# First stage of an embedding, filter and expert kernel: gathers taken straight from the index table, in another order against the graph vectors

## The chip, the cores and the metric

The kernel runs on one core of a Trainium2 chip. Its time is the device time of one execution in microseconds (us), and lower is better. The core has a matrix engine (PE), a vector engine (DVE), an activation engine (ACT), GpSimd (POOL), which here issues the gathers, and SyncE (SP), which issues plain transfers. Each works through its own list of instructions in order. They meet only at semaphores: an instruction signals one when it is complete, and a waiting instruction holds up everything behind it on its engine. 16 DMA engines move the data that SP, ACT and POOL ask for.

## The reference

64 sequences of 128 tokens pass through a token and graph embedding with a layer norm, a long convolution, and a layer of eight experts with two chosen per token. Only the first stage is touched by the change. For each sequence:

```python
emb = word_emb[input_ids] + pos_emb                  # 128 x 192
def vgcn(ids, adj, W, b):                            # three graphs
    ev = word_emb[ids]                               # 128 x 192
    H = einsum('bgh,bhd->bgd', adj, ev)
    g = H.mean(axis=1)                               # a mean over the 128 rows
    return relu(g @ W.T + b)                         # 16 values
x = concat([emb, graphs broadcast over the tokens])  # 192 + 48
y = layernorm(x @ W_proj.T + b_proj) * gamma + beta  # 192
```

The mean of `adj @ ev` over its rows is the vector of column means of `adj`, times `ev`; the kernel computes it so. Later stages use `y` of all sequences.

## The kernel before

The first stage works in 16 groups of four sequences (`NQ = 16`, `Q = 4`), numbered 0 to 15 here, with two buffers `p` for everything that a group holds. A group needs 16 gathers of 128 rows each: four for the tokens (`emb_g`, L473) and four for each of the three graphs (`ev_g`, L478), so twelve. It also needs three plain loads of adjacency matrices (`adj_s`, L358).

PE does for a group, in this order: twelve products of an adjacency matrix with a column of 1/128, which give its column means (L560, signal `colsum`); eight transposes of the gathered token rows (L565, L566, signal `emb_t`); twelve products of a diagonal-like block of the means with the gathered graph rows, summed into a 12 x 192 tile (L575, signal `gvec`: the graph vectors); two small transposes of that tile (L580, L581, signal `gt`); the graph features (L585, signal `gfeat`); the projection (L592, L593, signal `proj`).

ACT copies between these steps: the means onto the diagonals (L759, waits `colsum`), the turned embeddings (L762, L763, waits `emb_t`), the graph vectors (L768) and their transposes (L770, L771), then the relu (L773). It also normalizes rows of a group (L780, after `ln_ready`), splits the weights of one expert per two groups into a high part (L787, L788) and stores the split weights (L324). DVE waits for `proj` and then does two layer norms of the group (`rows`, L977 to L993, signal `ln_ready`), with a drain (a wait for its own earlier writes) between dependent steps, and computes the low part of an expert (L999, L1000) once per two groups. SP loads the adjacency of group i+2 once `colsum` of group i is signalled, and the next expert's weights once the last store has landed.

POOL first waits for `gvec` of group i-2, copies the group's indices out of the table with one instruction (L469, from `ids_i` into `idx`), and then issues all 16 gathers of group i. Groups 0 and 1 have no wait. After group 15 the Toeplitz tiles of the convolution are loaded into the room of `ev_g` (SP waits for `gvec` of all groups, L391), and the convolution (L611) starts when ACT has written the rows of the last group.

## Time and profile before

| | |
|---|---|
| median of three runs | 1231.76 us (1229.6 to 1235.03) |
| the profiled execution | 1239.12 us, its span 1237.3 us |
| granted clock of PE in the span | 0.816 of full speed |
| PE, DVE, ACT, POOL busy in the span | 71%, 52%, 44%, 54% |
| first stage | from the start to about 513 us, where L611 begins |

The profiled execution is 7.4 us longer than the median of the runs shown. A row of a timeline gives start, duration, engine, line, operation, output and input with their count, and in brackets how long the engine was idle before it and what ended that. Ends of matrix products are modelled, so a row of PE tells when the product was started, and the row of whoever waits for it tells when its signal was there. "remote" means that the profile could not tie the end of a wait to an instruction that had just ended.

### The profile page before, as it was taken

The numbers are of one execution on the slowest core, as the hardware profiler recorded it, in microseconds if no ns is written. First come the engines' busy times: TensorE is split into PE (matmuls) and PEld (weight loads), VectorE is DVE, ScalarE is ACT, GpSimd is POOL, SyncE is SP. The second block draws the span as 40 slices with busy tenths as digits, with TensorE's granted clock in tenths as the row PEclk, the third lists the DMA queues.
The fourth block names the chain that finished last, engine by engine and source line by source line (L and its number), as shares of the span: only waits on it lengthen the run. The fifth ranks groups of instructions, "written<-read, shape, count | busy, mean of one in ns | idle before, by whom it ended". The sixth has DMA issues, their size and how long they took to land. (4 is left out here: it accounts for less than half of the span.)

```text
span 1237.3 us, 22985 instructions
## 1 busy us (share of the span) xinstructions
PE 878.2 (71%) x7442; PEld 775.1 (63%) x7442; DVE 639.1 (52%) x2223; ACT 540.3 (44%) x1323; POOL 674.0 (54%) x608
## 2 busy tenths in 40 slices
PE   1544444654444547495875799998988998999991
PEld 0433333443333435495874689998988998998991
DVE  2043434453534354537868745664655565655661
ACT  1021212121212123354855757665655766676760
POOL 6455554655554650002530057776866887878874
PEclk9966666666666667696556989998999999999996
DMA  6234343543535351591088054477477446434442
GB/s 202 74 106 143 108 143 116 147 156 96 163 87 168 95 178 36 144 285 55 1 233 270 3 169 80 59 169 178 57 176 213 62 94 162 62 56 62 62 52 30
DMA packets 119542, 146.94 MB, mean 119 GB/s; under 512 B 13476, under 2 KB 105799, under 8 KB 117415
## 3 DMA queue, kind: packets, MB, share of 16 engines
q0 software_dynamic: 39552, 53.26, 23.1%
q1 hardware_dynamic: 78902, 82.31, 21.8%
q10 hardware_dynamic: 1008, 10.34, 2.1%
q8 instruction: 46, 0.75, 0.3%
q14 instruction: 34, 0.27, 0.1%
HBM read 107.05 MB, written 38.82 MB: 118 GB/s over the span
## 5 line engine op out<-in xcount | busy, mean ns | idle before, releaser
L880 ACT ACTIVATE Hs<-bank,U 128x256 bf16<-128x256 f32 x426 | 211.9, 497 | 183.7 <-PE bank L708 154.0
L517 POOL DMA_INDIRECT out<-Hs,si x142 | 236.9, 1669 | 85.5 <-issue 85.2
L1202 DVE TENSOR_TENSOR Hs<-Hs 128x512 bf16<-128x512 f32 x213 | 147.5, 692 | 148.2 <-ACT Hs L881 134.5
L575 PE MATMUL bank<-ev_g,diag 128*12 128x192 f32 x384 | 96.1, 429 | 179.8 <-ACT diag L759 172.1
L478 POOL DMA_INDIRECT ev_g<-in_word_emb,idx x192 | 185.0, 964 | 58.5 <-issue 58.5
L508 POOL DMA_INDIRECT blob<-xtab_d,gi x142 | 149.0, 1049 | 123.5 <-DVE gi L1187 84.2
L881 ACT ACTIVATE Hs<-bank,U 128x256 f32<-128x256 f32 x426 | 214.0, 502 | 0.0
L723 PE MATMUL bank<-U,Hs 128*128 128x192 bf16 x852 | 213.0, 250 | 0.2 <-issue 0.2
L725 PE MATMUL bank<-U,Hs 128*128 128x192 bf16 x852 | 211.4, 248 | 0.0
L724 PE MATMUL bank<-U,Hs 128*128 128x192 bf16 x852 | 211.1, 248 | 0.0
L575 PEld LDWEIGHTS bank<-ev_g,diag 128*12 128x12 f32 x384 | 44.0, 118 | 231.7 <-issue 119.5
L759 ACT ACTIVATE diag<-bank 128x12 f32<-128x12 f32 x16 | 3.1, 192 | 275.1 <-remote 270.0
L704 PE MATMUL bank<-blob,U 128*128 128x256 bf16 x426 | 117.0, 275 | 1.6 <-DVE blob L1191 1.6
L706 PE MATMUL bank<-blob,U 128*128 128x256 bf16 x426 | 116.9, 274 | 0.0
L705 PE MATMUL bank<-blob,U 128*128 128x256 bf16 x426 | 116.9, 274 | 0.0
L707 PE MATMUL bank<-blob,U 128*128 128x256 bf16 x426 | 116.9, 274 | 0.0
L708 PE MATMUL bank<-blob,U 128*128 128x256 bf16 x426 | 116.9, 274 | 0.0
L724 PEld LDWEIGHTS bank<-U,Hs 128*128 128x128 bf16 x852 | 84.9, 100 | 0.2
L723 PEld LDWEIGHTS bank<-U,Hs 128*128 128x128 bf16 x852 | 83.9, 98 | 0.7 <-issue 0.4
L725 PEld LDWEIGHTS bank<-U,Hs 128*128 128x128 bf16 x852 | 83.6, 98 | 0.2
L977 DVE TENSOR_TENSOR ys<-bank,posb 128x384 f32<-128x384 f32 x32 | 16.3, 552 | 127.4 <-PE bank L593 117.7
L473 POOL DMA_INDIRECT emb_g<-in_word_emb,idx x64 | 62.4, 974 | 31.2 <-issue 19.6
(184 smaller groups left out, 1726.5 us busy)
## 6 DMA issues: line engine op xcount, KB each, us to landing
U<-blob_d SPq DMA_DIRECT2D x20, 771.0 KB
U<-blob_d SPq DMA_DIRECT2D x20, 672.0 KB
adj_s<-in_adj SPq DMA_DIRECT2D x48, 256.0 KB
ev_g<-kpad_d SPq DMA_DIRECT2D x24, 512.0 KB, 6.2
wst<-in_wsrc SPq DMA_DIRECT2D x8, 1344.0 KB
blob_d<-blob ACTq DMA_DIRECT2D x7, 1443.0 KB
xtab_d<-U SPq DMA_DIRECT2D x4, 1552.0 KB, 8.9
out<-Hs SPq DMA_DIRECT2D x4, 1536.0 KB, 10.9
```

The source lines that it names most:

```text
L478: pool.indirect_dma_start(ev_g[:, p, j, b, :], None, t["word_emb"], bass.IndirectOffsetOnAxis(ap=idx[:, p, k:k + 1], axis=0)).then_inc(ev_ ...
L508: pool.indirect_dma_start(xg_f[:, q % RX, h, :], None, xtab_d, bass.IndirectOffsetOnAxis(ap=gi[:, q % RX, h:h + 1], axis=0)).then_inc(xg_i ...
L517: pool.indirect_dma_start(out, bass.IndirectOffsetOnAxis(ap=si[:, q % RX, h:h + 1], axis=0), yo[:, q % RX, h, :], None, compute_op=ALU.add ...
L575: last = mm(bank[3][0:KG, 0:D], diag[:, p, k, :], ev_g[:, p, j, b, :], start=k == 0, stop=k == KG - 1)
L704: mm(ps, hi[:, a], x0, start=True, stop=False)
L705: mm(ps, hi[:, a], x2, start=False, stop=False)
L723: mm(ps, hh[w][:, f, n], hi[:, c], start=f == 0, stop=False)
L724: mm(ps, hh[w][:, f, n], lo[:, c], start=False, stop=False)
L725: last = mm(ps, hl[w][:, f, n], hi[:, c], start=False, stop=f == FC - 1)
L880: f(hh[w][:, d, :], ps, ACT.Gelu, bias=bi[:, d:d + 1])
L881: last = f(hf[w][:, d, :], ps, ACT.Gelu, bias=bi[:, d:d + 1])
L1202: last = v.tensor_tensor(hl[w][:, c:c + 2, :], hf[w][:, c:c + 2, :], hh[w][:, c:c + 2, :], ALU.subtract)
```

## The change

The gathers take their indices directly from `ids_i`; the copy L469 and its two semaphores are gone, and POOL's loop over groups is written out. In place of one wait ahead of the group's gathers there are three: token gathers of group i wait for `emb_t` of group i-2, the first graph's four wait for `gvec` of group i-2, and the ninth gather of the 16 waits for `gvec` of group i-1 and `ln_ready` of group i-2.

On PE the column means of group i+1 now stand ahead of the graph vectors of group i, and the order within a group is: turn the embeddings, column means of the next group, graph vectors, features, projection. The graph vectors are computed with the gathered rows as the stationary operand, 24 products with one moving column (L569, L570 of the changed kernel), which gives them already turned: the copy into `grow_s`, its two transposes and the `diag` tile go away. The second product takes the last 128 of the 192 columns, so `wg` is laid out anew, with zeros where nothing is wanted. Adjacency loads take 2 KB in a row per partition (four matrix rows), and `mean_w` has four columns so that one product gives the four sequences' sums.

```diff
-                pe.wait_ge(adj_in[p], 16 * GRAPHS * (it + 1))
+            def column_means(n, i, p):
+                pe.wait_ge(adj_in[p], 16 * GRAPHS * n)
+                after(pe, cs_ready, i)
                 for j in range(GRAPHS):
-                    for b in range(Q):
-                        k = p * KG + j * Q + b
-                        last = mm(bank[0][:, k:k + 1], adj_s[:, p, j, b, :], mean_w[:, :], start=True, stop=True)
+                    k = p * KG + j * Q
+                    for r in range(Q):
+                        last = mm(bank[0][:, k:k + Q], adj_s[:, p, j, r, :], mean_w[:, :], start=r == 0, stop=r == Q - 1)
                 last.then_inc(colsum, 1)
...
-                pe.wait_ge(diag_ready, i + 1)
+            def graph_vectors(it, i, p):
+                pe.wait_ge(cs_ready, i + 1)
+                after(pe, gfeat_ready, i)
                 pe.wait_ge(ev_in[p], 16 * KG * (it + 1))
...
-                        last = mm(bank[3][0:KG, 0:D], diag[:, p, k, :], ev_g[:, p, j, b, :],
-                                  start=k == 0, stop=k == KG - 1)
+                        mm(bank[3][:, k:k + 1], ev_g[:, p, j, b, 0:D0], cs[:, p, k:k + 1], start=True, stop=True)
+                        last = mm(bank[3][:, 16 + k:17 + k], ev_g[:, p, j, b, D - 128:D], cs[:, p, k:k + 1], start=True, stop=True)
...
             def pair(it):
                 for p in range(2):
-                    quad(it, p)
-
-            steps(pe, NQ // 2, pair)
+                    i = 2 * it + p
+                    turn_embeddings(it, i, p)
+                    if not (isinstance(i, int) and i == NQ - 1):
+                        column_means(it + 1 + p, i + 1, 1 - p)
+                    graph_vectors(it, i, p)
+                    graph_features(i)
+                    project(i, p)
```

On POOL, one group in its loop before, with the gathers of `emb_g` and `ev_g`:

```order
L469 ISA [waits gvec]
L469 COPY idx<-ids_i 128x16
L470 REGISTER_ALU
L473 DMA emb_g<-in_word_emb,idx 128x192 [waits idx_staged]
L473 DMA emb_g<-in_word_emb,idx 128x192 x3
L478 DMA ev_g<-in_word_emb,idx 128x192 x12
```

and one group of the changed kernel, which is written out for every group:

```order
L464 DMA emb_g<-in_word_emb,ids_i 128x192 [waits emb_t]
L464 DMA emb_g<-in_word_emb,ids_i 128x192 x3
L472 DMA ev_g<-in_word_emb,ids_i 128x192 [waits gvec]
L472 DMA ev_g<-in_word_emb,ids_i 128x192 x3
L472 DMA ev_g<-in_word_emb,ids_i 128x192 [waits ln_ready,gvec]
L472 DMA ev_g<-in_word_emb,ids_i 128x192 x7
```

The place at which POOL holds for graph vectors moves from ahead of the first gather of group i to ahead of its ninth, and the group waited for there is i-1, not i-2.

On ACT, the odd group of a pair in the loop before, from its first copy to the relu:

```order
L759 ACTIVATE diag<-bank 128x12 [waits colsum]
L762 ACTIVATE xt<-bank 128x512 [waits proj,emb_t]
L763 ACTIVATE xt<-bank 64x512
L786 ISA
L787 ACTIVATE blob<-wst 128x1536 [waits w_in]
L788 ACTIVATE blob<-wst 128x1152
L768 ACTIVATE grow_s<-bank 12x192 [waits gvec]
L770 ACTIVATE gt_s<-bank 128x12 [waits gt]
L771 ACTIVATE gt_s<-bank 64x12
L773 ACTIVATE xt<-bank,gbias 48x512 [waits gfeat]
```

and in the changed kernel, from its first copy to the split of the expert's weights:

```order
L762 ACTIVATE xt<-bank 128x512 [waits proj,emb_t]
L763 ACTIVATE xt<-bank 64x512
L755 REGISTER_ALU
L757 ACTIVATE cs<-bank 128x12 [waits gvec,colsum]
L767 ACTIVATE gt_s<-bank 128x12 [waits gvec]
L768 ACTIVATE gt_s<-bank 128x12
L770 ACTIVATE xt<-bank,gbias 48x512 [waits gfeat]
L783 ISA
L784 ACTIVATE blob<-wst 128x1536 [waits w_in]
L785 ACTIVATE blob<-wst 128x1152
```

The copy of the means stands behind the embedding copies and belongs to the next group, and the split of the expert's weights has moved from ahead of the graph vectors to behind the relu.

## Rows read from the trace of the kernel before

**Rows 1.** The line of POOL's wait for graph vectors: count, min/median/max ns, first and last start.

```profile
L469 POOLq FUSED_REGOPS  x14: 46/46/58, 56.0 to 442.7; - x14
```

**Rows 2.** Timeline of POOL, group 4: start us, us, instruction, idle time before it.

```profile
117.63 0.20 POOL L469 COPY idx<-ids_i 128x16 int32 x1 [9.69 <-PE bank L575]
118.65 0.98 POOL L473 DMA_INDIRECT emb_g<-in_word_emb,idx  x1 [0.82 <-POOL idx L469]
...
137.78 0.95 POOL L478 DMA_INDIRECT ev_g<-in_word_emb,idx  x1 [0.30 <-issue]
```

**Rows 3.** Timeline of PE, group 3.

```profile
123.21 2.73 PE L560 MATMUL bank<-mean_w,adj_s 128*128 128x1 f32 x24
...
141.84 6.28 PE L575 MATMUL bank<-ev_g,diag 128*12 128x192 f32 x24 [14.15 <-ACT diag L759]
```

**Rows 4.** Timeline of ACT, group 3.

```profile
141.60 0.19 ACT L759 ACTIVATE diag<-bank 128x12 f32<-128x12 f32 x1 [19.03 <-remote]
141.71 0.60 ACT L762 ACTIVATE xt<-bank 128x512 f32<-128x512 f32 x1
...
142.68 1.47 ACT L787 ACTIVATE blob<-wst 128x1536 bf16<-128x1536 f32 x1
```

**Rows 5.** DMA share in 40 slices of 135 to 143 us, in tenths.

```profile
DMA  0006630009631002942000932000000000000006
```

**Rows 6.** Timelines of ACT and PE, group 15, while no gather runs.

```profile
483.52 0.19 ACT L759 ACTIVATE diag<-bank 128x12 f32<-128x12 f32 x1 [5.09 <-PE bank L560]
484.35 5.71 PE L575 MATMUL bank<-ev_g,diag 128*12 128x192 f32 x24
```

**Rows 7.** Timelines of group 6: POOL, then PE, then ACT, then DVE.

```profile
210.70 0.98 POOL L473 DMA_INDIRECT emb_g<-in_word_emb,idx  x1 [0.82 <-POOL idx L469]
213.53 0.97 POOL L473 DMA_INDIRECT emb_g<-in_word_emb,idx  x1 [1.85 <-issue]
235.34 0.20 POOL L469 COPY idx<-ids_i 128x16 int32 x1 [3.20 <-remote]
236.36 0.98 POOL L473 DMA_INDIRECT emb_g<-in_word_emb,idx  x1 [0.82 <-POOL idx L469]
...
222.47 6.92 PE L575 MATMUL bank<-ev_g,diag 128*12 128x192 f32 x24 [2.81 <-ACT diag L759]
...
235.03 0.60 ACT L762 ACTIVATE xt<-bank 128x512 f32<-128x512 f32 x1 [12.69 <-remote]
236.00 0.30 ACT L768 ACTIVATE grow_s<-bank 12x192 f32<-12x192 f32 x1
236.79 0.18 ACT L770 ACTIVATE gt_s<-bank 128x12 f32<-128x12 f32 x1 [0.48 <-PE bank L581]
...
238.69 0.68 ACT L773 ACTIVATE xt<-bank,gbias 48x512 f32<-48x512 f32 x1 [1.66 <-PE bank L585]
...
245.01 1.02 DVE L977 TENSOR_TENSOR ys<-bank,posb 128x384 f32<-128x384 f32 x2 [6.94 <-PE bank L593]
264.10 0.16 DVE L993 SCALAR_TENSOR_TENSOR ln<-mv,ln 128x4 f32<-128x4 f32 x1
```

**Rows 8.** Timeline of DVE, rows of group 2, then the expert.

```profile
123.41 1.02 DVE L977 TENSOR_TENSOR ys<-bank,posb 128x384 f32<-128x384 f32 x2 [8.98 <-PE bank L593]
...
140.13 0.38 DVE L966 BATCH_NORM_AGGREGATE mv<-stats 128x2 f32<-128x6 f32 x4 [3.82 <-issue]
145.00 0.16 DVE L993 SCALAR_TENSOR_TENSOR ln<-mv,ln 128x4 f32<-128x4 f32 x1
145.33 1.76 DVE L999 TENSOR_TENSOR blob<-wst,blob 128x1536 bf16<-128x1536 f32 x1 [0.16 <-ACT blob L788]
```

**Rows 9.** Timeline of DVE, rows of group 15.

```profile
497.28 1.02 DVE L977 TENSOR_TENSOR ys<-bank,posb 128x384 f32<-128x384 f32 x2 [2.56 <-PE bank L593]
...
510.95 0.16 DVE L993 SCALAR_TENSOR_TENSOR ln<-mv,ln 128x4 f32<-128x4 f32 x1
```

**Rows 10.** Timeline of PE at the start of the stage.

```profile
36.09 5.25 PE L560 MATMUL bank<-mean_w,adj_s 128*128 128x1 f32 x24 [7.19 <-issue]
```

More of the change, by code:

```diff
@@ L132, in tower @@
         adj_s = sb("adj_s", [128, 2, GRAPHS, Q, 128])
-        grow_s = sb("grow_s", [KG, D])
         gt_s = sb("gt_s", [128, 2, KG])
@@ L340, in _ @@
             load(scale_shift[:, :], t["gamma_beta"].partition_broadcast(128))
-            for c, rows in ((0, D0), (1, D1)):
-                own = bass.AP(tensor=wg, offset=c * GRAPHS * GRAPHS * GD,
-                              ap=[[2 * GRAPHS * GRAPHS * GD, rows], [(GRAPHS + 1) * GD, GRAPHS], [1, GD]])
+            pitch = 2 * GRAPHS * 128
+            for c, first, rows in ((0, 0, D0), (1, 128 - D1, D1)):
+                own = bass.AP(tensor=wg, offset=first * pitch + c * GRAPHS * 128 + D1,
+                              ap=[[pitch, rows], [128 + GD, GRAPHS], [1, GD]])
                 load(own, t["WgT"][c * D0:c * D0 + rows, :].rearrange("d (j g) -> d j g", j=GRAPHS))
@@ L597, in pair @@
                 for p in range(2):
-                    quad(it, p)
-            steps(pe, NQ // 2, pair)
+                    i = 2 * it + p
[5 more added lines that the diff above has]
+                    project(i, p)
+            column_means(1, 0, 0)
+            steps(pe, NQ // 2, pair, last=1)
             pe.wait_ge(rows_done, NQ)
@@ L752, in _, with column_copy, embedding_copy @@
             f(dec[0:D1, 1, :], trow[0:D1, :], ACT.Exp, scale=filt[0:D1, 1, 3:4]).then_inc(dec_done, 1)
[L754 to L755 removed]
+            def column_copy(i, p):
                 act.wait_ge(colsum, i + 1)
[L758 to L759 removed]
+                after(act, gvec, i - 1)
+                f(cs[:, p, :], bank[0][:, p * KG:(p + 1) * KG], ACT.Copy).then_inc(cs_ready, 1)
+            def embedding_copy(i, p):
                 act.wait_ge(emb_t, i + 1)
@@ L790, in pairs @@
             def pairs(it):
-                quad(it, 0)
-                graphs(it, 0)
-                if not (isinstance(it, int) and it == 0):
-                    normal(2 * it - 1, 1)
-                quad(it, 1)
-                split_hi(it)
-                graphs(it, 1)
-                normal(2 * it, 0)
+                for p in range(2):
+                    i = 2 * it + p
+                    embedding_copy(i, p)
+                    if not (isinstance(i, int) and i == NQ - 1):
+                        column_copy(i + 1, 1 - p)
+                    graphs(i, p)
+                    if p:
+                        split_hi(it)
+                    if not (isinstance(i, int) and i == 0):
+                        normal(i - 1, 1 - p)
                 if not (isinstance(it, int) and it > 0):
                     store_expert(act, it)
+            column_copy(0, 0)
             steps(act, NQ // 2, pairs, last=1)
@@ L856, in _ @@
             gap_exp(NG - 1)
-            f(junk[:, :], mean_w[:, :], ACT.Gelu)
+            f(junk[:, :], mean_w[:, 0:1], ACT.Gelu)
             def hots(it):
```

81 lines of the change are left out of this document (33 added, 48 removed).

## The prediction

> **What bounds the first stage now.** I read first how often POOL comes to its wait for graph vectors, then the timelines of POOL, PE and ACT over one group, then the DMA share behind the last gather, then the two places where the pattern differs. The later stages are not touched, so only the first one can move.
>
> The 14 waits of POOL lie between 56.0 and 442.7 us [rows 1]. That is 386.7 us for 13 groups, 29.75 us a group. POOL's own work is less: from the first gather at 118.65 to the end of the last at 138.73 it needs 20.1 us, and between blocks it stands for 9.69 us until PE's L575 is done [rows 2]. So the stage is a ring: graph vectors, 16 gathers, something, graph vectors.
>
> The something is the odd part. PE started the column means of group 3 at 123.21; they are over at 125.94, the transposes follow at once, and then PE had no work for 14.15 us [rows 3]. Yet ACT, which waits for the means, got their signal only at 141.60, and that of the transposes right after, at 141.71 [rows 4]. The copy then ran 0.2 us, and L575 could begin. The last DMA traffic of the gathers is at 135 + 25 x 0.2 = 140.0 us, and nothing moves before 142.8 [rows 5]. In group 15, with no gather running, the same signal is there as soon as L560 is over: the copy starts at 483.52 and its wait is ended by L560 itself, not by "remote" [rows 6]. I take it so: while gathers run, PE's completion signals are held, and they come out when the gathers have been still for some 1.5 us. From the first gather of a block of 16 to that release is 141.60 - 118.65 = 22.95 us. With L575's 6.28 us, the step to POOL and the index copy (118.65 - 117.63 = 1.02), this gives the 30.7 us of an ordinary group.
>
> Group 6 checks it. There the means came out early, and L575 ran inside the block, from 222.47 to 229.39. POOL and ACT still saw its signal only at about 235 [rows 7]. So finished graph vectors are held too. The gathers had started at 210.70 and lost 1.55 us to a late second one, and the next block started at 236.36: 25.66 us a group.
>
> The page Perfetto Trace Analysis of the Trainium skill (Tensor Engine Instruction) says that the end shown for a matmul is computed, and that the signal goes out once PSUM has acknowledged the writes. The trace agrees that the two can lie apart, here by some 14 us.
>
> **What the change does, part by part.** In the changed kernel the wait is inside the group, but from wait to wait there are still 16 gathers: eight of group i+1 and eight of group i+2. They go out in one run. Behind the waiting ninth gather stand the group's other seven and all later gathers.
>
> *Means a group ahead.* Graph vectors no longer need a round trip within their own block. The rows of group i+1 are complete after the first eight gathers: 8 x 1.27 + 1.3 = 11.5 us into the block (spacing 19.13/15 [rows 2], 1.3 from the end of the last gather to the end of traffic [rows 5]). The 24 products have 128-row weights and one column, as L560's twelve with 2.73 us [rows 3], so 5.5 us; not below that, and at most L575's rate, 12.6 us. They end 17 us into the block, or 24 at worst. I take 5.5, the alike row. By the signal rule the result is seen at 22.95, so 5.5 costs nothing and the worst 1 us, which the next term hides. The adjacency loads and the copies of the means have a whole group of slack, so their new shape is worth 0.
>
> *Index copy, grow_s, two transposes.* The copy took 1.02 us of every ring and now goes. The detour over `grow_s` took 236.79 - 236.00 = 0.79 us [rows 7].
>
> *What is late next: DVE.* The ninth gather also waits for `ln_ready` of the group whose projection falls into the block. Without gathers, rows of a group take 511.11 - 497.28 = 13.8 us [rows 9]. Beside gathers they took 145.16 - 123.41 = 21.75 [rows 8], because the drains stand: 3.82 us ahead of L966 alone. Counted from the first gather at 118.65, DVE began at 4.8 us and was done at 26.5. In the block that began at 236.36 it began at 8.65 and was done at 27.9 [rows 7]. The end hardly depends on the beginning, as DVE's last big drain ends with the release.
>
> When does DVE begin in the changed kernel? At the release ACT finds three signals at once, as in group 6, and copies the embeddings first. From the graph vectors' signal (235.34) to L977 (245.01) it took 9.7 us there, less the detour 8.9. In odd groups DVE computes the expert's low part before the rows, since ACT's split now stands behind the relu. The relu ended at 239.37, 4.0 us after the vectors' signal [rows 7], less the detour 3.2; the split's first piece takes 1.47 us [rows 4] and the second, with three quarters of the columns, 1.1; the low part 1.76 [rows 8] and 1.3 by the same share. That makes 8.8, nearly the same. Let d be how long the block starts after the graph vectors' signal. Then DVE begins at 8.9 - d and ends at 26.4 for 4.8 or 27.9 for 8.65, plus 0.3 for POOL's restart. With d = 3.8: DVE begins at 5.1, ends at 26.5, next block at 26.7 to 26.8, and d = 3.8 again. So the ring is 26.7 us, set by the layer norm, and not 22.95 + 0.3 = 23.2, set by graph vectors.
>
> *Start and end.* Before, graph vectors 0 were signalled at 56.0 [rows 1]. Now POOL stops after 24 gathers, at about 34 us, before PE's first means at 36.09 [rows 10]. PE then does 5.25 of means, 1.8 of transposes, 2.7 of the next means, and 5.5 to the vectors: 52 us. The last block has only eight gathers, so nothing is held: group 15's vectors come 11.5 + 5.5 = 17 us after its start. Before, L575 of group 15 ended at 490.1 [rows 6]. What follows (projection, rows, rows out to the convolution) stays.
>
> *The sum.* 52 + 14 x 26.7 + 17 = 442.8 us instead of 490.1, so 47 us less. POOL's code is now written out; a fetch gap like the 1.55 us of [rows 7] costs between 0 and 1.55 a block, and it sits in the 29.75 now too, so I take 0. From the execution of 1239.1 this gives 1192; that execution lay 7.4 us above the median of the runs, so the forecast is 1184 us, with 1165 to 1200 if the ring is 25.5 to 28 us.
>
> **Rivals.** *Graph vectors set the ring (23.2 us).* If DVE's drains stall less when rows begin earlier, the layer norm is done before the release. For it: 13.8 us of rows from 5.1 would be 19. Against it: every drain behind a large write from some 10 us into the block was slow. Sum: 52 + 325 + 17 = 394, so 96 us less: 1136. Chance 0.16.
>
> *Signals are not held by gathers.* If something else holds them, graph vectors are seen at 17 us, POOL never stands, and the ring is its 16 gathers, 20.2 us: 52 + 283 + 17 = 352, so 138 less: 1094. The group that shows held graph vectors speaks against it [rows 7]. The page SBUF — State Buffer of the Trainium skill (SBUF: two separate sides) has a rule for this side: PE, ACT and DVE's own ports never wait on anyone, only the pair shared by DVE and GpSimd blocks. By it 14.15 us of PE should not hang on gathers; the trace disagrees. Chance 0.04.
>
> *The projection's signal is held too.* In one block it came through at 8.65 us [rows 7], but that of the means of [rows 3], over 7.3 us after the first gather, did not. In the changed kernel it comes at 8.9 when d is 0. If it is held to 22.95, rows end at 22.95 + 13.8 = 36.8, the next block starts that late, and its own projection is then over before it begins. Rings of 36.8 and 23.2 alternate, 30.0 on average: 52 + 420 + 17 = 489, so 1 us less, 1230: no change. Chance 0.08.
>
> *The same without the recovery: slower.* The place is DVE's wait for the projection. If ACT, held up behind the layer norm and the expert's store (which waits for DVE's low part), gets to the embedding copies only after the next block has begun, each block's projection is held and each ring is 36.8 us: 52 + 515 + 17 = 584, so 94 more: 1326. For it: ACT's list now has split, normalizing and store in a row ahead of the next copies. Against it: those copies wait for a signal that comes at the release anyway. It decides from a mean ring of 30.1 us, where the sum reaches 490. Chance 0.07.
>
> *A ring of 28 to 30 us*, from expert transfers that fall among the gathers and move the release: 52 + 14 x 28.5 + 17 = 468, so 22 less: 1210. Chance 0.07.
>
> **How the numbers follow.** The forecast's own case has 0.58. The range reaches down to the vectors' ring, 1136, and up over most of the slow rings: 1135 to 1214. Out of it lie the unheld ring, no change and slower, 0.19 together. A change of 0.5%, 6 us, is about what measurement can tell from none. Faster by more: 0.58 + 0.16 + 0.04 + 0.07, and 0.03 of the alternating case, so 0.88; within: 0.05; slower: 0.07.
>
> **What the profile will show.** If I am right, POOL's idle ahead of a ninth gather recurs every 26 to 27 us and is 5 to 6.5 us long, ended by DVE's L996 and not by PE. L570 is started about 17 us into a block while ACT's L767 starts 23 to 24.5 us into it, so that the signal is held as before. Rows of a group still take 21 us or so. Graph vectors 0 are there at 52. Wrong would be: POOL idle for under 3 us ended by PE (vectors' ring), no idle (unheld), or DVE waiting for the projection past 20 us into a block (held projection).

## The result, and the profile after

| | before | changed |
|---|---|---|
| median (7 runs each, one chip) | 1233.43 us (1229.6 to 1235.52) | 1224.85 us (1220.7 to 1229.37) |
| ratio, 95% interval | | 0.9936 (0.9911 to 0.9961) |
| profiled execution, its span | 1239.12, 1237.3 us | 1229.37, 1227.2 us |
| granted clock of PE in the span | 0.816 | 0.792 |

The change gains 8.6 us, 0.6% of the time. The forecast was 47 us less than before, and its range began at 1135 and ended at 1214, so the time lies above it. The profiled execution shows the same miss: it was to be 1192 and is 1229.

Who ends POOL's wait at the ninth gather (the line of the changed kernel's graph gathers: count, min/median/max ns, first and last start; below it, idle us, times):

```profile
L472 POOL DMA_INDIRECT ev_g<-in_word_emb,ids_i x192: 944/949/2431, 8.3 to 465.7; - x192
  PE bank L570: 136.0, 15
```

It was to be DVE's L996, the end of the layer norm. It is L570, the last of the graph-vector products, all 15 times. The first, three middle ones and the last of these waits, on POOL's timeline (answers to [rows 1, 2]):

```profile
61.91 0.95 POOL L472 DMA_INDIRECT ev_g<-in_word_emb,ids_i  x1 [28.75 <-PE bank L570]
...
118.37 0.95 POOL L472 DMA_INDIRECT ev_g<-in_word_emb,ids_i  x1 [4.52 <-PE bank L570]
...
148.54 0.95 POOL L472 DMA_INDIRECT ev_g<-in_word_emb,ids_i  x1 [10.44 <-PE bank L570]
...
174.53 0.95 POOL L472 DMA_INDIRECT ev_g<-in_word_emb,ids_i  x1 [4.82 <-PE bank L570]
...
456.91 0.94 POOL L472 DMA_INDIRECT ev_g<-in_word_emb,ids_i  x1 [4.83 <-PE bank L570]
```

I call the 16 gathers from one of these waits to the next a block, and the time from one block's first gather to the next one's a ring. Rings alternate: 30.2 us from 118.37 to 148.54, 26.0 us from there to 174.53. The mean of all 14 is (456.91 - 61.91)/14 = 28.2 us, against 29.75 before and 26.7 forecast. The seven long ones are 30.2 us on average and the seven short ones 26.2, so all that the rings took beyond the forecast was taken by the long ones.

PE in the short ring and at the start of the stage. The second fence answers to [rows 3, 10]. The count behind the x is of records; each product has two records, and I call the time from one record's start to the next one's a pass:

```profile
158.44 2.74 PE L551 MATMUL bank<-mean_w,adj_s 128*128 128x4 f32 x24
163.76 0.59 PE L569 MATMUL bank<-cs,ev_g 128*128 128x1 f32 x2 [2.57 <-issue]
...
173.69 0.57 PE L570 MATMUL bank<-cs,ev_g 128*128 128x1 f32 x2
```

```profile
39.42 5.25 PE L551 MATMUL bank<-mean_w,adj_s 128*128 128x4 f32 x24 [3.25 <-DVE kT L943]
...
46.28 5.12 PE L551 MATMUL bank<-mean_w,adj_s 128*128 128x4 f32 x24
51.26 0.57 PE L569 MATMUL bank<-cs,ev_g 128*128 128x1 f32 x2
...
61.07 0.56 PE L570 MATMUL bank<-cs,ev_g 128*128 128x1 f32 x2
```

The 24 products, 48 passes, take 174.26 - 163.76 = 10.5 us in the ring and 61.63 - 51.26 = 10.4 us at the start. A pass is 0.21 us. The means in the same ring have 24 records in 2.74 us, so 0.114 us a pass, and the first means of the stage 5.25, so 0.219. Windows give start:end, us, then the busy time and records of PE, PEld, DVE, ACT and POOL, the granted clock, the DMA share and GB/s. The first three are the means, the pause and the products of the short ring; the next two are the means and the first products of the long ring, where there is no pause; the last is the products at the start:

```profile
158.40:161.10 2.70, 2.70 (x26) 2.70 (x24) 2.30 (x13) 1.07 (x2) 1.90 (x2) 1.00 1.02 410
161.10:163.70 2.60, 0.08 (x1) 0.00 (x0) 1.85 (x10) 0.00 (x0) 1.94 (x3) 0.53 0.92 285
163.80:174.00 10.20, 10.06 (x48) 10.18 (x48) 6.30 (x30) 0.18 (x1) 4.69 (x5) 0.50 0.87 285
```

```profile
128.10:130.80 2.70, 2.70 (x26) 2.70 (x25) 2.38 (x12) 1.07 (x2) 1.90 (x2) 0.95 0.27 76
130.80:133.20 2.40, 2.40 (x12) 2.40 (x12) 1.24 (x9) 0.00 (x0) 1.89 (x2) 0.50 0.31 82
```

```profile
51.26:61.40 10.14, 10.14 (x49) 10.14 (x49) 0.00 (x0) 0.18 (x1) 0.00 (x0) 1.00 0.25 79
```

In the short ring PE runs the means at full clock (granted 1.00, 2.4 GHz); in the pause the granted clock is 0.53, and in the 10 us of products behind it 0.50 (1.2 GHz). The long ring has no pause, and there too the products stand at 0.50 right behind means at 0.95. The price isn't fixed, though: the first four products of group 1, from 73.43 to 74.3 us, took 0.11 us a pass at a granted 1.00.

The long ring, PE and ACT (answers to [rows 3, 4]):

```profile
128.08 2.87 PE L551 MATMUL bank<-mean_w,adj_s 128*128 128x4 f32 x24
...
132.94 0.35 PE L570 MATMUL bank<-cs,ev_g 128*128 128x1 f32 x1
...
135.29 0.16 PE L570 MATMUL bank<-cs,ev_g 128*128 128x1 f32 x1 [2.00 <-issue]
...
140.91 0.38 PE L570 MATMUL bank<-cs,ev_g 128*128 128x1 f32 x2 [1.94 <-issue]
...
147.55 0.57 PE L570 MATMUL bank<-cs,ev_g 128*128 128x1 f32 x2
```

```profile
128.29 0.60 ACT L762 ACTIVATE xt<-bank 128x512 f32<-128x512 f32 x1 [4.23 <-PE bank L559]
...
141.13 0.18 ACT L757 ACTIVATE cs<-bank 128x12 f32<-128x12 f32 x1 [11.77 <-remote]
148.15 0.18 ACT L767 ACTIVATE gt_s<-bank 128x12 f32<-128x12 f32 x1 [6.84 <-PE bank L570]
```

The means are over at 130.9, ACT gets their signal at 141.1, 22.8 us after the block's first gather: the release of [rows 4], at the place where it was expected. What was not expected is PE itself. It begins the products at 130.8 and, from 133.3 to 140.9, gets only three records off ("issue" is time in which it waited for nothing that the profile shows). So under the gathers not only PE's signals are late but its instructions too. The other sign, finished graph vectors held back, is not there: the last product ends at 148.1, and L767 starts at 148.15.

In the short ring the release needed no stand of the gathers. The means were over at 161.2 and ACT had their signal at 165.85, while gathers were issued without a break from 148.54 to 169.7:

```profile
165.85 0.18 ACT L757 ACTIVATE cs<-bank 128x12 f32<-128x12 f32 x1 [6.06 <-remote]
```

DVE's rows of a group in the long and in the short ring, first and last instruction (answers to [rows 7, 8]):

```profile
127.41 1.02 DVE L980 TENSOR_TENSOR ys<-bank,posb 128x384 f32<-128x384 f32 x2 [10.58 <-issue]
...
147.60 0.16 DVE L996 SCALAR_TENSOR_TENSOR ln<-mv,ln 128x4 f32<-128x4 f32 x1
...
157.54 1.02 DVE L980 TENSOR_TENSOR ys<-bank,posb 128x384 f32<-128x384 f32 x2
...
172.98 0.16 DVE L996 SCALAR_TENSOR_TENSOR ln<-mv,ln 128x4 f32<-128x4 f32 x1
```

They begin 9.0 us into either block, where the forecast had 5.1, and end 29.4 and 24.6 us into it, only 0.8 and 1.4 us ahead of the next block's first gather. So they take 20.4 us in the long ring, about the 21 of the forecast, but 15.6 in the short one.

### The profile page after: what moved, and what is told of

It is laid out like the page before. It is cut to its first block and busy times, and to the rows that moved or that the text cites. A ratio compares the mean times of both kernels' runs of the same rounds, so it can differ in the third digit from the quotient of the medians.

```text
span 1227.2 us, 23628 instructions
## 1 busy us (share of the span) xinstructions
PE 977.4 (80%) x7794; PEld 936.0 (76%) x7794; DVE 642.8 (52%) x2233; ACT 536.4 (44%) x1307; POOL 673.4 (55%) x592
## 3 DMA queue, kind: packets, MB, share of 16 engines
q1 hardware_dynamic: 60470, 82.31, 21.5%
## 5 line engine op out<-in xcount | busy, mean ns | idle before, releaser
L472 POOL DMA_INDIRECT ev_g<-in_word_emb,ids_i x192 | 193.3, 1007 | 190.0 <-PE bank L570 136.0
L569 PE MATMUL bank<-cs,ev_g 128*128 128x1 f32 x384 | 105.5, 341 | 53.3 <-issue 40.3
L569 PEld LDWEIGHTS bank<-cs,ev_g 128*128 128x128 f32 x384 | 103.1, 325 | 55.0 <-issue 43.8
L570 PE MATMUL bank<-cs,ev_g 128*128 128x1 f32 x384 | 105.7, 342 | 26.7 <-issue 26.4
L570 PEld LDWEIGHTS bank<-cs,ev_g 128*128 128x128 f32 x384 | 103.7, 326 | 22.2 <-issue 22.2
L724 PEld LDWEIGHTS bank<-U,Hs 128*128 128x128 bf16 x852 | 83.9, 99 | 0.1
L723 PEld LDWEIGHTS bank<-U,Hs 128*128 128x128 bf16 x852 | 82.8, 97 | 0.5 <-issue 0.4
L725 PEld LDWEIGHTS bank<-U,Hs 128*128 128x128 bf16 x852 | 82.7, 97 | 0.1
```

Source lines behind the costliest of these rows:

```text
L472: pool.indirect_dma_start(ev_g[:, p, j, b, :], None, t["word_emb"], bass.IndirectOffsetOnAxis(ap=ids_i[:, 1 + j, i * Q + b:i * Q + b + 1], ...
L569: mm(bank[3][:, k:k + 1], ev_g[:, p, j, b, 0:D0], cs[:, p, k:k + 1], start=True, stop=True)
L570: last = mm(bank[3][:, 16 + k:17 + k], ev_g[:, p, j, b, D - 128:D], cs[:, p, k:k + 1], start=True, stop=True)
L723: mm(ps, hh[w][:, f, n], hi[:, c], start=f == 0, stop=False)
L724: mm(ps, hh[w][:, f, n], lo[:, c], start=False, stop=False)
L725: last = mm(ps, hl[w][:, f, n], hi[:, c], start=False, stop=f == FC - 1)
```

## The experiments

"Before" was timed on the same chip each time. It took 1096 to 1102 us on eight of the ten chips met, and 1234 and 1237 us on the two others, like the chip of the prediction. I call the eight free chips and the others holding chips, for what the traces taken on them show. Ratios are to before on the same chip.

| kernel | free chips | holding chips |
|---|---|---|
| changed kernel | 1.0451 (1.042 to 1.0482) | 0.9936 (0.9911 to 0.9961) |
| old products, ninth wait kept | 1.0146 (1.0097 to 1.0196); 1.0126 (1.0054 to 1.0199) | 0.9723 (0.969 to 0.9756) |
| thin products, no ninth wait | 1.0133 (1.0106 to 1.0159) | not run |
| old products, no ninth wait | 0.9868 (0.9827 to 0.9908) | 0.9422 (0.9361 to 0.9484) |
| before, index table alone | 0.9823 (0.9778 to 0.9869) | not run |

Each of the three holding ratios is from another time or chip, so differences between rows are differences between ratios.

**The kernel before on a free chip** (c1_before, no edit).

> The kernel before, unchanged, for a trace of it on the chip that runs the other three. Theory H (PE's signals are held on some chips only): where its time is near 1230 us the ring of the first stage is 29.8 us and ACT's L759 starts some 22.9 us after a block's first gather; where it is near 1097 us the signal of the means is there about 12.5 us into the block, POOL never stands for graph vectors, and the ring is its 16 gathers and the index copy, 20 to 21.5 us. Rival K (the signals are held by this kernel's own order, and the chips differ elsewhere): L759 comes at 22.9 us on either chip and the difference lies behind the first stage.

1098.93 us in one run. PE and ACT of the same part of the stage, then POOL's index copy of a later group:

```profile
102.64 3.02 PE L560 MATMUL bank<-mean_w,adj_s 128*128 128x1 f32 x24
...
115.78 6.27 PE L575 MATMUL bank<-ev_g,diag 128*12 128x192 f32 x24 [9.19 <-DMA ev_g<-in_word_emb,idx]
```

```profile
105.70 0.19 ACT L759 ACTIVATE diag<-bank 128x12 f32<-128x12 f32 x1 [3.18 <-PE bank L560]
```

```profile
131.41 0.21 POOL L469 COPY idx<-ids_i 128x16 int32 x1
```

L759 follows the means at once, in the midst of gathers (in [rows 4] it came 15.7 us after their end). POOL has no idle time ahead of L469: it doesn't stand for graph vectors there, nor ahead of any other copy. L469's waits lie between 37.1 and 316.4 us, so the ring is 279.3/13 = 21.5 us, not 29.75, and the convolution L611 starts at 379.7 and not 513.4 us. That is 133.7 of the 140.2 us between the spans. Theory H holds, rival K falls: the kernel is the same, and the chips differ almost only in this one stage.

**The changed kernel on a free chip** (c2_after, no edit).

> The changed kernel, unchanged. Theory H: on a chip that holds signals 0.994 of before, rings of 30.2 and 26.1 us. On one that does not, POOL's ring of before has no standing time, while in the changed kernel the ninth gather still waits for the 24 thin products at half clock: rings near 24 us, so some 3 us x 14 more than before, and the start some 5 us later: ratio 1.04 to 1.05, slower. Rival K: 0.99 to 1.00 on any chip.

1.0451: slower, as theory H has it. POOL's waits in it, the two groups that matter:

```profile
L472 POOL DMA_INDIRECT ev_g<-in_word_emb,ids_i x192: 941/947/2024, 8.3 to 392.4; - x192
...
  PE bank L570: 42.1, 8
  DVE ln L996: 25.4, 7
```

POOL, which never stood before, stands 67.5 us. That is more than the 49 us by which the kernel is slower; the index copies, worth 20 us in a run below, are gone.

**Old products, wait kept** (e1_old_products, f1_old_products and g1_old_products are one kernel on three chips). The copies into `diag`, `grow_s` and `gt_s` that belong to the old products are back on ACT too; the cut shows PE's part.

```diff
-  mm(bank[3][:, k:k + 1], ev_g[:, p, j, b, 0:D0], cs[:, p, k:k + 1], start=True, stop=True)
-  last = mm(bank[3][:, 16 + k:17 + k], ev_g[:, p, j, b, D - 128:D], cs[:, p, k:k + 1], start=True, stop=True)
+  last = mm(bank[3][0:KG, 0:D], diag[:, p, k, :], ev_g[:, p, j, b, :], start=k == 0, stop=k == KG - 1)
...
+  nc.tensor.transpose(bank[0][:, 64:64 + KG], grow_s[:, D - 128:D], ident[0:KG, 0:KG])
+  nc.tensor.transpose(bank[0][:, 32:32 + KG], grow_s[:, 0:D0], ident[0:KG, 0:KG]).then_inc(gt, 1)
```

> The changed kernel with the graph vectors computed in the old form again: twelve products of 192 columns into a 12 x 192 tile, the copy into grow_s, two transposes. Waits, order and everything else stay as changed. Theory T (the 24 thin products are the cost: 10.3 us at half clock in place of the 5.5 us that I forecast): the old form needs 6.3 us plus 0.8 for the detour, so rings of 26.1 us shrink to 23 to 24 and those of 30.1 to 27 or less; over 14 rings 35 to 45 us less than the changed kernel, 1185 us. Theory H (signals and products of PE are held while gathers run with no other traffic, whatever the products are): the rings of about 30 us stay above 29 and only the others shrink, 10 to 20 us less than the changed kernel, 1205 to 1215 us.

> The changed kernel with graph vectors as before (twelve products of 192 columns, grow_s, two transposes), the ninth gather's wait kept: the same kernel as e1_old_products, for another chip. On a chip that does not hold signals it is 1.015 of before again. On one that does (before near 1235 us) the changed kernel is 0.994 and the one with neither thin products nor the wait 0.942. Theory P (the thin products are what the forecast mis-sized): graph vectors take 6 us in place of 10 and no PE stall falls into them, the rings are 26 to 27 us, ratio 0.955 to 0.965, most of the way down. Rival W (the wait is what costs): rings of 28 us stay, 0.985 to 0.995.

> The changed kernel with the old graph-vector products and the ninth gather's wait kept, once more for another chip. No held signals: 1.013 to 1.015 of before again. Held (before near 1235 us; changed kernel 0.994, neither thin products nor wait 0.942): theory P (the thin products are what the forecast mis-sized) 0.955 to 0.965, rings of 26 to 27 us; rival W (the wait is what costs) 0.985 to 0.995.

The first two met free chips, the third (1199.31 us, 0.9723) a holding one. It lies between the two theories' numbers, and its trace tells why. Its graph-vector products, its waits, and the ends of the first and the last of them:

```profile
210.38 6.31 PE L573 MATMUL bank<-ev_g,diag 128*12 128x192 f32 x24 [4.43 <-issue]
```

```profile
L476 POOL DMA_INDIRECT ev_g<-in_word_emb,ids_i x192: 942/946/2400, 8.3 to 445.2; - x192
...
  DVE ln L1008: 92.2, 14
  issue: 53.9, 177
  PE bank L573: 27.1, 1
```

```profile
60.19 0.94 POOL L476 DMA_INDIRECT ev_g<-in_word_emb,ids_i  x1 [27.14 <-PE bank L573]
...
436.50 0.94 POOL L476 DMA_INDIRECT ev_g<-in_word_emb,ids_i  x1 [4.70 <-DVE ln L1008]
```

With graph vectors that cost 6.3 us and not 10.5, the layer norm (L1008 here) ends all 14 waits that follow the first, and the mean ring is (436.50 - 60.19)/14 = 26.9 us. That the layer norm is the last waiter is the forecast's mechanism. That the mean is within 0.2 us of its 26.7 is partly luck, for the rings still alternate, between some 25 and 28.5 us, which the forecast did not have. In the ring from 115.30 to 144.04, DVE's rows began 8.1 us into the block and ended 28.0 us into it, in the next one 7.3 and 24.2, where the forecast had 5.1 and 26.5 for every block. The kernel's profiled execution took 1199.95 us where the forecast had 1192.

**Thin products, no ninth wait** (e5_no_ninth_wait).

```diff
                 for j in range(GRAPHS):
-                    if j == 1:
-                        after(pool, gvec, i)
-                        after(pool, ln_ready, i - 1)
```

> The changed kernel without the wait of the ninth gather for graph vectors of the preceding group and ln_ready; the buffers stay guarded by emb_t and gvec of group i-2. If the wait is what costs (theory W): on a chip without held signals the ring falls from 24 to between 20 us (POOL's 16 gathers) and 22 us (PE's own work of a group at half clock), ratio to before 0.99 to 1.02 and 25 to 50 us below the changed kernel; on a chip that holds signals POOL would pause only when its gathers of group i+2 meet graph vectors i, ring 26 to 30 us. If it is PE's products at half clock (theory P): the ring stays near 24 us, within 8 us of the changed kernel, with POOL waiting for gvec at its fifth gather in place of the ninth.

1117.29 us, 1.0133: 34 us below the changed kernel on the same chip. That is theory W's size, but theory P has its share, since the case that lacks the thin products too is 0.9868. The rings are 21.6 us on average, and PE is busy in 226.7 of the 240 us between 110 and 350: what is left is near to PE's own work.

**Neither** (e7_old_no_wait and g7_old_no_wait are one kernel: both edits above, without thin products and without the ninth wait).

> The changed kernel with two of its parts undone: graph vectors as before (twelve products of 192 columns, grow_s and its two transposes), and no wait of the ninth gather for gvec of the preceding group and ln_ready. What is left is the direct index table, the means a group ahead and the long adjacency rows. Theory W (wait and thin products are the two costs, each alone leaving 1.013 to 1.015 of before): with neither, POOL's 16 gathers are the ring, 20.2 us, ratio 0.975 to 0.985 as with the index table alone (0.982). Rival: another part, the means ahead or the new order on ACT, costs as well, ratio 0.99 to 1.01. If this chip holds PE's signals while gathers run (before near 1230 us), the ring is 22.95 us and what POOL needs to start again, 0.3, or up to 26.7 where the layer norm or PE are later: ratio 0.92 to 0.96.

> The kernel of e7_old_no_wait (changed kernel, old graph-vector products, no wait of the ninth gather), for another chip. Held signals (before near 1235 us): 0.94 again. No held signals: by theory W+P (wait and thin products are the only two costs) POOL's 16 gathers set the ring, 20.2 to 20.7 us, and the ratio is 0.975 to 0.99, about that of the index table alone (0.982). Rival M: the means a group ahead cost too, since their 2.7 us stand between the turned embeddings and the graph vectors, and POOL's fifth gather comes to wait: ring 21.5 us, 0.99 to 1.005.

e7 met a holding chip: 1165.25 us, 0.9422, rings of 24.3 us on average ((373.2 - 56.7)/13, first gathers of groups 2 and 15), within what was expected. g7 met a free one: 1085.63 us, 0.9868. There POOL's line has no waits but its own issue gaps, so its gathers are the ring (20.7 us on average):

```profile
L473 POOL DMA_INDIRECT ev_g<-in_word_emb,ids_i x192: 945/949/2512, 8.4 to 331.6; - x192
...
  issue: 58.5, 192
```

On a free chip (1100 us) the wait costs 0.026 to 0.032 of before, 29 to 35 us, and the thin products nearly the same, whichever one takes away first; rival M falls. 12 us of the wait's cost is paid once, at the start: the ninth gather of group 1 goes out at 45.45 us in e1 and at 33.51 in g7. On a holding chip the wait costs 0.030 (with the old products) and the thin products 0.021 (with the wait), 37 and 26 us of 1235. These differences are between ratios taken on different chips, except for the wait's 0.032 with thin products, where both kernels ran on one.

e7 has something more. POOL stands at other places in it, so that there are runs of 16 and of 12 gathers. The last gather before two of its stands, and what ACT got then:

```profile
257.03 0.95 POOL L468 DMA_INDIRECT emb_g<-in_word_emb,ids_i  x1 [0.30 <-issue]
260.49 0.95 POOL L473 DMA_INDIRECT ev_g<-in_word_emb,ids_i  x1 [2.51 <-remote]
...
274.26 0.95 POOL L473 DMA_INDIRECT ev_g<-in_word_emb,ids_i  x1 [0.30 <-issue]
277.90 0.95 POOL L468 DMA_INDIRECT emb_g<-in_word_emb,ids_i  x1 [2.69 <-remote]
```

```profile
246.80 0.60 ACT L768 ACTIVATE xt<-bank 128x512 f32<-128x512 f32 x1 [2.00 <-PE bank L560]
...
260.25 0.32 ACT L773 ACTIVATE grow_s<-bank 12x192 f32<-12x192 f32 x1 [7.20 <-remote]
...
277.67 0.60 ACT L768 ACTIVATE xt<-bank 128x512 f32<-128x512 f32 x1 [10.64 <-remote]
```

The release comes 2.3 us after the last gather's end (260.25 - 257.98) and 2.5 us (277.67 - 275.21), once 23.5 us after the run's first gather (236.75) and once 17.2 (260.49). So in these two the release goes with the stand of the gathers, and not with how long ago they began. But a stand isn't the only release: the turned embeddings got through at 246.80, 10 us into a run, and the means, over at 249.2, at 252.85, in the midst of it, as the changed kernel's at 165.85. What decides which signals are held to the end of a run stays open.

**The index table alone** (e6_before_direct): before, with the copy L469 gone, indices from `ids_i` and the loop written out.

```diff
-                if not (isinstance(i, int) and i < 2):
-                    pool.wait_ge(gvec, i - 1)
-                nc.gpsimd.tensor_copy(idx[:, p, :]..., ids_i[:, :, bass.ds(i * Q, Q)]).then_inc(idx_staged, 1)
-                pool.wait_ge(idx_staged, i + 1)
-                pool.sem_inc(pool_turn, 1)
+                after(pool, gvec, i - 1)
...
-                                            bass.IndirectOffsetOnAxis(ap=idx[:, p, b:b + 1], axis=0)).then_inc(emb_in[p], 16)
+                                            bass.IndirectOffsetOnAxis(ap=ids_i[:, 0, i * Q + b:i * Q + b + 1], axis=0)).then_inc(emb_in[p], 16)
```

> The kernel before, but the gathers take their indices straight from ids_i, the index copy L469 is gone and POOL's loop is written out; every order and wait else stays. The copy and its semaphores cost 1.02 us a group. On a chip whose ring is POOL's own work, 14 to 16 us less than before, ratio 0.985 to 0.988. On a chip that holds signals the copy is in the ring as well, ratio 0.987 to 0.99. Rival: the written-out loop costs fetch gaps of up to 1.5 us a group, which eat the gain: 0.995 to 1.005.

1082.28 us, 0.9823 (0.9778 to 0.9869): as expected or a little better. This part of the change is a gain by itself on a free chip, and no fetch gap eats it.

**A pause among the gathers** (e8, f8, g8, h8, i8 and j8_thirteenth_pause are one kernel): e6 with a wait ahead of the thirteenth gather.

```diff
+                    if j == 2:
+                        after(pool, colsum, i)
```

> The kernel before with indices straight from ids_i, and one wait more: ahead of the last four of a group's 16 gathers POOL waits for the column means that PE makes during that group. Theory H: on a chip with no held signals the means are there some 13 us into the block, before the thirteenth gather is due at 15.2 us, the wait costs nothing, and the ratio is that of the index table alone, 0.98 to 0.985. On a chip that holds signals (before near 1230 us) POOL pauses at 15 us, the signals come out at 17.8, graph vectors are computed during the last four gathers, and the ring falls from 29.7 to 26.1 us: some 50 us less, ratio 0.94 to 0.96. Rival (the holding has nothing to do with the gathers standing still): on such a chip the pause itself is added to the ring, ratio 0.99 to 1.02.

> The kernel of e8_thirteenth_pause, for another chip. No held signals: 0.984 of before again. Held (before near 1235 us): POOL stands at 15 us into a block for the means, they come out at 17.8, the ring is 26.1 us and the ratio 0.94 to 0.96; if a pause of the gathers does not let signals out, 0.99 to 1.02.

> The kernel of e8_thirteenth_pause, for another chip. No held signals: 0.984 to 0.987 of before again. Held (before near 1235 us): POOL stands at 15 us into a block for the means, they come out at 17.8, the ring is 26.1 us and the ratio 0.94 to 0.96; if a pause of the gathers does not let signals out, 0.99 to 1.02.

> The kernel of e8_thirteenth_pause once more for another chip. No held signals: 0.984 to 0.987 of before again. Held (before near 1235 us): POOL stands at 15 us into a block for the means, they come out at 17.8, the ring is 26.1 us and the ratio 0.94 to 0.96; if a pause of the gathers does not let signals out, 0.99 to 1.02.

> The kernel of e8_thirteenth_pause once more for another chip. No held signals: 0.984 to 0.987 of before again. Held (before near 1235 us): POOL stands at 15 us into a block for the means, they come out at 17.8, the ring is 26.1 us and the ratio 0.94 to 0.96; if a pause of the gathers does not let signals out, 0.99 to 1.02.

> The kernel of e8_thirteenth_pause once more for another chip. No held signals: 0.984 to 0.987 of before again. Held (before near 1235 us): POOL stands at 15 us into a block for the means, they come out at 17.8, the ring is 26.1 us and the ratio 0.94 to 0.96; if a pause of the gathers does not let signals out, 0.99 to 1.02.

All six met free chips: 0.9841, 0.9871, 0.9849, 0.9865, 0.9863 and 0.9846. That is the ratio of the index table alone within its interval. So the wait costs nothing that these runs can show there, and what it would do on a holding chip wasn't seen. That a stand of the gathers lets signals out rests on the ends of the runs in before's, the changed kernel's and e7's traces; a stand put in for that purpose stays untried.

**More columns between the thin products** (e2_more_columns): 15 idle products of 192 columns a group, written to room that nobody reads. Four stand among the column means, six ahead of the graph vectors and five among them; the cut shows the five.

```diff
+                        if k % 2 == 1 and k < KG - 1:
+                            mm(bank[3][:, 300:492], ident[:, :], wp0[:, :], start=True, stop=True)
```

> The changed kernel with 15 products more per group whose result nobody reads (128 weights, 192 columns, into unused columns of a bank): four among the column means, six ahead of the graph vectors, five among them. They are pure extra work of about 0.33 us each at full clock. Theory C (the graph vectors run at half clock because one-column products do not keep the clock up): the granted clock over the rings rises from 0.60 to over 0.75, the pass of a graph vector product from 0.213 to about 0.11 us, and the rings do not get longer, 0 to 30 us less than the changed kernel. If the clock is not raised by columns: the pass stays at 0.213 us and the rings grow by 3 to 6 us, 40 to 80 us more.

1184.56 us, 1.0822 (1.0747 to 1.0897), a free chip. From 110 to 350 us the granted clock was 0.72, and 0.61 in c2_after. The records of the thin products, which overlap, last 0.28 us on average and not 0.337. From 150.0 to 153.8 us the clock is 1.00 and a thin pass takes 0.11 us; from 154.2 to 159.3, in the same group, it is 0.50 and 0.21. So the pace goes with the granted clock, and theory C's clock of over 0.75 wasn't reached. The added products took more than that gave back: the rings are 25.5 us on average, from 23.0 to 27.4, against 23.9 in c2_after.

**Expert transfers** (e3_small_expert, e4_extra_store): fewer and more bytes beside the gathers. e3 loads and stores only 8 columns of experts 1 to 6 in the stage and writes full blocks behind it, so it leaves out the split weights of these experts. e4 adds 1.38 MB of stores in each even group, and ACT's loop is written out for it.

```diff
-            eng.dma_start(blob_d[bass.ds(e, 1), :, :]..., blob[:, :]).then_inc(w_out, 16)
+            w = BLOB if isinstance(e, int) and e in (0, E - 1) else 8
+            eng.dma_start(blob_d[bass.ds(e, 1), :, 0:w]..., blob[:, 0:w]).then_inc(w_out, 16)
```

```diff
+                        for n in range(7):
+                            act.dma_start(extra_d[n, :, :], scale_shift[:, :]).then_inc(extra, 16)
```

> The changed kernel, but in the first stage experts 1 to 6 load and store only 8 of their columns (the split weights of these experts are therefore not the reference's); blocks of the full size are written after the stage instead, so only the first stage is to be compared. Theory H (PE's signals and products are held when the gathers run alone, and not when other traffic runs beside them): the short rings of 26.1 us, which are those with the expert's transfers, become like the others, about 30 us, so less traffic makes the stage longer by up to 25 us. Theory T (traffic only delays the gathers): the short rings get shorter, as the graph rows land 3.6 us earlier, 22 to 25 us.

> The changed kernel with 1.38 MB of stores more from a constant tile, issued by ACT in each even group behind its normalizing, so that the rings of about 30 us get DMA traffic beside the gathers too; ACT's loop is written out for it. Theory H (gathers alone hold PE back, other traffic releases it): the rings of 30 us fall to 26 to 27, so more work makes the kernel 15 to 25 us faster than the changed one, 1200 to 1210 us. Theory T (it is the products' length): rings stay or grow by the delay of the gathers, 0 to 20 us more.

e3 took 1176.36 us in one run, its stores behind the stage included; e4 1151.2 us, 1.0478 (1.0448 to 1.0508), near the changed kernel's 1.0451 on another free chip. The DMA share between 110 and 350 us was 0.36 in e3, 0.59 in e4 and 0.51 in c2_after, and the rings are 24.0 us on average in all three (first gathers of groups 2 and 15). So on a free chip expert transfers don't set the ring. Whether they make the long and short rings alternate on a holding one, where the traces put them in step, this pair could not tell.

## Why the prediction was wrong

**The ring before and who sets it** was read right. Before's time came again on the two holding chips of the experiments, and on a free chip the same kernel, whose signals aren't late there, has the 21.5 us that POOL's own work makes.

**The step that failed is the price of the 24 thin products.** I wrote "I take 5.5, the alike row", from L560's 2.73 us in [rows 3], and put at most 12.6. They took 10.5. The row for it stood in the prediction's own [rows 10]: the same 24 records of L560 at 5.25 us, so 0.219 us a pass, 48 passes 10.5 us. I had used that row for the start and not asked at which of the two paces the products would run. The sum also let the worst price pass at 1 us, hidden by the layer norm; that held only with products begun 11.5 us into the block. In the short ring they began 163.76 - 148.54 = 15.2 us into it, so 15.2 + 10.5 is 25.7 and the next block at 26.0. Why so late is argued: rows of the eighth gather may land later beside expert traffic (DMA share 0.92 there and not the 0.27 of the long one), but the profile puts this pause down to the gathers' rows in only three of the seven short rings, and to "issue" in four. g1 shows the step by itself: with products of 6.3 us the layer norm is the last waiter again, the long rings fall from 30.2 to 28.1 us on average, the short ones from 26.2 to 25.7, and the ratio is 0.9723 and not 0.9936.

**The price came back through d.** The forecast's ring rests on d = 3.8 us between the vectors' signal and the next block, in which PE gets the projection ready. With vectors that set the ring, d is 0.3, and by the prediction's own 8.9 - d DVE begins 8.6 us into the block; it was 9.0. For a beginning at 8.65 the forecast had the end at 27.9, and in long rings it is 29.4, in short ones 24.6. So dear products moved both waiters: the vectors end the short ring at 26.0 themselves, and the rows, 4 us late, fill the long one. A second reading failed here, that the rows end at about the same place in every block: behind the same beginning their ends lie 4.8 us apart in the two kinds of ring, and g1 has this too (28.0 and 24.2). The traces show no steady ring of 26.7, and why the rings alternate stays open.

**Held issue was no term.** In long rings PE lost 7.6 us in the midst of the products. I had taken from [rows 3] that PE works on under the gathers and only its signals are late. Held issue set only the last 0.4 us of a long ring, for L996 ended at 147.76 and the vectors' signal came at 148.15; what the same holding did to DVE's rows is in their 20.4 us.

**The sum, term by term**, from the changed kernel's own execution:

| | forecast | measured |
|---|---|---|
| graph vectors 0 | 52 us | 61.6 (61.91 less 0.3) |
| 14 rings | 373.8 (26.7 each) | 395.0 (28.2 each) |
| last block | 17 | 22 (L570 of group 15 ends at 478.9) |
| sum | 442.8 | 479 |

The difference, 36 us, is nearly all of the profiled execution's 1229 against 1192: 9.6 from the start, 21.2 from the rings and 5 from the last block. The rings alone would have left the forecast at 1206, within its range. In the last block the dear products are the whole difference: they began 11.7 us into it, near the 11.5 of the forecast (468.58 in the trace). At the start, the first means came 3.3 us late (they wait for DVE's `kT`), the second took 5.12 for 2.7, and the products 10.4 for 5.5: the slow pace twice more. The granted clock of that window is 1.00 and still a pass takes 0.21 us, so the column would not have warned.

**The rivals.** "Graph vectors set the ring" named the right waiter, but had it at 23.2 us because it shared the price. "The projection's signal is held too" had alternating rings and 1230 us, near the 1224.85 by luck: it held the projection to 22.95 us into a block, and DVE began at 9.0 in either kind. The ring of 28 to 30 us, which is where the mean came out (28.2), had 0.07, and expert transfers for its cause; products at half clock and held issue are what the traces show. "Signals are not held", with 0.04, is what eight of ten chips do, and its ring of 20.2 with no stand of POOL was wrong too: on those chips the changed kernel has rings of 24 us and is 4.5% slower. The prediction set against this rival a rule from SBUF — State Buffer of the Trainium skill (SBUF: two separate sides), that PE's own ports never wait on anyone, and said that the trace disagrees. That went too far: the traces of the holding chips show late signals and late issue, but none shows a port that waits, so they neither bear the rule out nor refute it.

**Where the gain went.** The index table alone is worth 20 us on a free chip (e6). There, the ninth gather's wait costs 29 to 35 us and the thin products 29 to 35 us; the old ring had neither, since POOL was two groups ahead. On a holding chip POOL stood anyway, the kernel with neither is 72 us faster than before, and the two costs take 63 of these back. How much of the 72 is the index table and how much the means a group ahead, no run on a holding chip separates. The kernel of e7 and g7 beats both kernels on both kinds of chip; the index table alone is about as good on a free one (0.9823 against 0.9868, with intervals that overlap).

What holds PE's signals and instructions on some chips stays open. The runs tie it to the time in which gathers go out and to the chip, for the same kernel has it on one chip and not on another.

## What to carry to other kernels

Where a trace has the same product at two paces, as L560 at 0.114 and 0.219 us a pass here, carry both through the sum, and don't take the nearer row alone. A one-column product took the slow pace in these rings with and without a wait ahead of it. A wait that buys order (here, graph vectors ahead of the ninth gather) isn't free because its engine stands anyway: it cost 37 us where POOL stood in the kernel before too, and 29 to 35 where it didn't. Find out whether an engine stands for the kernel's reasons or for those of one chip, by running before on another. When a sum lets a doubtful price hide under the next term, work out the sum with both ends.

## What the runs showed of the hardware

One kernel took 1096 to 1102 us on eight chips and 1233 to 1237 us on the others, with 134 of the 140 us between two traces in the stage with indirect gathers. On the slower chips PE's signals, PE's issue and DVE's steps stall under a run of gathers. In the long rings of before and of the changed kernel and in e7's two stands, the signal comes 2.3 to 3.1 us after the end of the run's last gather; in short rings it also comes in the midst of a run (165.85). DVE's rows of a group took 21.75 us beside gathers in before and 13.8 in c1_before (L977 at 103.30 to the end of L993 at 117.13), as long as with no gather running in before [rows 9]. Of the waits of PE's products that are put down to "issue" (waited for: us, times, longest), c2_after on a free chip has none from 100 to 330 us, and the changed kernel on the chip of the prediction has, from 100 to 400 us:

```profile
PE bank L569 <- issue: 27.3, 14, 3.1
PE bank L570 <- issue: 19.0, 12, 2.6
```

Granted clock and speed of a pass can disagree: 1.00 with 0.213 us a pass from 51.3 to 61.4 us, as at 0.50 later. TensorE: Matmul & The Clock Gate of the Trainium skill (Seeing it yourself) warns that the clock's trace events have been seen to be unreliable, and this window agrees. A gather whose issue met DVE's two-input step on the expert (L1002, 1.76 us at 154.49) took 2.27 us for 0.95. The changed kernel's trace has seven gathers of over 1.3 us between 40 and 480 us, 2.27 to 2.43 us long, and they are the seven that met L1002:

```profile
154.80 2.27 POOL L472 DMA_INDIRECT ev_g<-in_word_emb,ids_i  x1 [0.31 <-issue]
```
